# Second layer of a two-layer metaformer: the softplus chain, the convolution taps and the B/C eviction move to other steps of ScalarE's turn, and the gate's matmul uses the convolution's bank

## The reference, cut to what matters

```
xz = einsum('bhwc,ec->bhwe', xp, in_proj_w)          # x_in and x_gate, 96 channels each
x_act = silu(conv3x3_depthwise(x_in))                # two-dimensional
# _mamba(x_act):
xm, z = split(x_act @ in_w)                          # 96 channels each
xm = silu(conv1d_depthwise(xm, 3 taps) + c1_b)
dt_r, Bm, Cm = split(xm @ xp_w)
dt = softplus(dt_r @ dt_w + dt_b);  A = -exp(A_log)
h[t] = exp(dt*A) * h[t-1] + (dt*xm) * Bm             # 16 states per channel
y = (sum over states of h*Cm + xm*D) * silu(z)
out = einsum((y @ out_w) * silu(x_gate), out_proj_w)
```

## Time and profile before

| | |
|---|---|
| median of 3 runs | 1864.99 us (1864.54 to 1865.83) |
| the profiled execution's own time | 1864.62 us |
| its span on the core | 1862.8 us |
| scans of the phase | first starts at 937.8 us, last at 1697.4 us |
| mean granted TensorE clock | 0.791 of full speed |

### The profile page before, as it was taken

How to read it: one execution, slowest core, us unless ns; L and a number is a source line. 1 busy time by engine, 2 the same in 40 slices (tenths; PEclk the granted TensorE clock), 3 DMA queues, 4 the chain that set the end, 5 groups by cost and what they waited for, 6 DMA issues and landing times. The chain is left out here.

```text
span 1862.8 us, 16204 instructions
## 1 busy us (share of the span) xinstructions
PE 1396.1 (75%) x4014; PEld 522.0 (28%) x4014; DVE 1346.9 (72%) x1217; ACT 1124.8 (60%) x1720; POOL 937.7 (50%) x430
## 2 busy tenths in 40 slices
PE   4499937455474188884888988888888888765996
PEld 3233300101001067762222222222222222110785
DVE  1255529999999445552078999999999999995575
ACT  3333327647476055563677888888887887741464
POOL 4100015958859300000387888888888888861000
PEclk9799955555555599996778888888888888865898
DMA  5323340020110213221466777767666667641562
GB/s 135 105 78 94 94 123 21 2 90 0 47 45 0 96 39 85 70 66 48 110 157 165 166 167 167 166 157 164 163 161 163 158 159 164 144 110 43 135 166 72
DMA packets 136006, 199.98 MB, mean 107 GB/s; under 512 B 27244, under 2 KB 69486, under 8 KB 134771
## 3 DMA queue, kind: packets, MB, share of 16 engines
q1 hardware_dynamic: 134522, 196.61, 42.1%
q10 hardware_dynamic: 1416, 2.61, 0.5%
HBM read 145.55 MB, written 53.63 MB: 107 GB/s over the span
## 5 line engine op out<-in xcount | busy, mean ns | idle before, releaser
L1650 DVE TENSOR_TENSOR_SCAN m_h<-m_qa,m_state,m_ub 128x512 f32<-128x512 f32 x384 | 464.0, 1262 | 53.9 <-ACT m_qa L1613 53.9
L1261 POOL TENSOR_TENSOR m_ub<-m_dlb,m_bt 128x1536 f32<-128x1536 f32 x128 | 439.1, 3439 | 17.4 <-DVE m_h L1650 14.4
L1613 ACT ACTIVATE m_qa<-m_dlb,k_a 128x512 f32<-128x512 f32 x384 | 250.3, 678 | 110.3 <-DVE m_h L1650 110.0
L1022 POOL TENSOR_TENSOR b_u<-b_dl,b_z 128x1024 f32<-128x1024 f32 x48 | 125.7, 2618 | 272.1 <-DVE b_dl L952 272.1
L1470 PE MATMUL m_qc<-m_bcr,k_selc 32*128 32x512 f32 x256 | 172.7, 759 | 83.4 <-DVE m_g L1661 83.3
L1661 DVE TENSOR_TENSOR m_g<-m_h,m_qc 128x1536 f32<-128x1536 f32 x128 | 222.4, 1737 | 15.2 <-DVE m_h L1650 8.8
L1486 PE MATMUL m_qy<-m_g,k_seld 128*32 128x512 f32 x768 | 170.3, 747 | 0.0
L887 PE MATMUL b_qc<-b_bc,k_pack_sel 96*128 96x512 bf16 x96 | 69.9, 824 | 127.3 <-DVE b_g L982 108.4
L1240 POOL MEMSET m_cva<- 128x640 f32 x2 | 1.3, 631 | 232.7 <-POOLq L1866 232.7
L968 DVE TENSOR_TENSOR_SCAN b_h<-b_da,b_h,b_u 128x1024 f32<-128x1024 f32 x36 | 118.0, 3278 | 0.0
L1405 PE MATMUL m_qf<-m_cva,k_conv 113*96 113x504 f32 (+1 forms) x192 | 94.9, 633 | 18.7 <-DMA m_cvb<-scratch_xpad 18.7
(11 more groups left out here) (179 smaller groups left out, 2804.2 us busy)
## 6 DMA issues: line engine op xcount, KB each, us to landing
m_dlb<-scratch_dldu SPq DMA_DIRECT2D x128, 384.0 KB, 10.2
m_bt<-scratch_brow SPq DMA_DIRECT2D x128, 256.0 KB, 6.0
scratch_dldu<-m_dldu SPq DMA_DIRECT2D x32, 384.0 KB, 3.1
scratch_z<-a_z SPq DMA_DIRECT2D x24, 256.0 KB, 4.5
b_z<-scratch_z SPq DMA_DIRECT2D x3, 2048.0 KB, 7.7
scratch_y<-b_yrow SPq DMA_DIRECT2D x3, 2048.0 KB, 6.3
c_y<-scratch_y SPq DMA_DIRECT2D x16, 384.0 KB, 3.3
scratch_gate<-m_gt SPq DMA_DIRECT2D x32, 192.0 KB, 5.0
```

Of the source, the lines that this page charges most:

```text
L1022: nc.gpsimd.tensor_tensor(by_column(u[s][:], col), by_column(dl[s][:], col), seen(z[:], col, piece), ALU.mult).then_inc(u_ready, 1)
L1261: nc.gpsimd.tensor_tensor(ub[k % 3][:], dlb[u % 2][:, J:2 * J, :], bcast(bt[u % 2][:, n, :], J), ALU.mult).then_inc(ub_ready, 1)
L1613: nc.scalar.activation(q_a[:, j, :], dlb[u % 2][:, j, :], ACT.Exp, scale=G["a1"][:, j, n:n + 1]).then_inc(da, 1)
L1650: nc.vector.tensor_tensor_scan(h[k % 3][:, j, :], q_a[:, j, :], ub[k % 3][:, j, :], state[:, k % NS, j:j + 1], ALU.mult, ALU.add).then_inc ...
```

## The change

The steps of the turn are dealt out anew. On ACT `log(t+3)` moves from s = 2 to s = 3, and `taps` and `rows_out` move from s = 3 of one turn to s = 0 of the next (so they are written with `t+3` and `t+2`), `rows_out` now ahead of `taps`. The SiLU of the gate moves behind the other three. The gate's matmul writes to `q_f`, the bank of the two-dimensional convolution, after its SiLU has read it (`xa_ready`), in place of `q_g`, the bank of `dt_of`. DVE's `softplus` moves from s = 0 to s = 1, ahead of `outputs`. POOL and SP follow with their parts.

```diff
 # POOL
             def step(t, s, k):
+                if s == 1:
+                    conv_sum(t + 3)
                 drive(k + 2)
-                if s == 3:
-                    rounding(t + 3)
                 if s == 0:
-                    conv_sum(t + 3)
-                if s == 1:
+                    rounding(t + 2)
+                if s == 2:
                     du_of(t + 2)
 # SP
             def step(t, s, k):
+                if s == 0:
+                    store_rows(t + 2)
                 if s == 1:
-                    store_drive(t + 2)
                     store_y(t - 1)
                     load_cv(t + 6)
                 if s == 2:
                     store_gate(t + 4)
+                    store_drive(t + 2)
                 if s == 3:
                     load_rows(t + 2)
                     load_drive(t + 2)
-                    store_rows(t + 3)
 # PE, conv_pairs, gate_of, dt_of
                 if v >= 1:
-                    pe.wait_ge(xa_ready, v)
+                    pe.wait_ge(gt_ready, v)
...
-                if v >= 1:
-                    pe.wait_ge(gt_ready, v)
-                if v >= 2:
-                    pe.wait_ge(delta, v - 1)
-                nc.tensor.matmul(q_g[:], G["l1_gate"][:], cva[v % 2][0:C, W:W + CH], start=True, stop=True).then_inc(gate_mm, 1)
+                pe.wait_ge(xa_ready, v + 1)
+                nc.tensor.matmul(q_f[:], G["l1_gate"][:], cva[v % 2][0:C, W:W + CH], start=True, stop=True).then_inc(gate_mm, 1)
...
-                pe.wait_ge(gt_ready, min(v + 2, UNITS))
+                if v >= 1:
+                    pe.wait_ge(delta, v)
                 nc.tensor.matmul(q_g[:], G["wdt"][:], xm[v % 4][:], start=True, stop=True).then_inc(dt_mm, 1)
 # ACT, window: the gate's SiLU behind sz and xm, from q_f
-                    act.wait_ge(gate_mm, a + 1)
-
-                    if a >= 2:
-                        act.wait_ge(gt_stored[a % 2], 16 * (a // 2))
-                    nc.scalar.activation(gt[a % 2][:], q_g[:], ACT.Silu).then_inc(gt_ready, 1)
...
+                if exists(a):
+                    act.wait_ge(gate_mm, a + 1)
+
+                    if a >= 2:
+                        act.wait_ge(gt_stored[a % 2], 16 * (a // 2))
+                    nc.scalar.activation(gt[a % 2][:], q_f[:], ACT.Silu).then_inc(gt_ready, 1)
 # ACT
                 if s == 2:
                     u_of(t + 4)
+                if s == 3:
                     log(t + 3)
-                if s == 3:
-                    taps(t + 4)
-                    rows_out(t + 3)
+                if s == 0:
+                    rows_out(t + 2)
+                    taps(t + 3)
 # DVE
             def step(t, s, k):
                 scans(k)
-                if s == 0:
+                if s == 1:
                     softplus(t + 2)
-                if s == 1:
                     outputs(t - 1)
                 times_c(k - 1)
```

## The result

| | before | after |
|---|---|---|
| median | 1864.76 us (1862.95 to 1865.83, 4 runs) | 1877.28 us (1875.42 to 1881.51, 4 runs) |
| profiled execution, its span | 1864.62, 1862.8 us | 1876.55, 1874.8 us |
| mean granted clock of the span | 0.791 | 0.781 |

The changed kernel takes 1.0071 times as long, 95% interval 1.0052 to 1.0090. It is slower, by 12.5 us where I had forecast 43.

The account below looks back on a forecast made before the run. DVE, nearest to full, was taken to be held by ACT's late decay. Removing that but delaying `z_of`, 22.04 + 1.30 + 2.0 for PE's clock gave 25.3 us a turn, 1.4 slower over 29 turns: 1908 us, range 1870 to 1945.

Parts of the forecast that it names:

- DVE's own turn of 22.04 us: On DVE, a turn's own work without waits was put at 22.04 us, against a measured turn of 23.88.
- The wait for the decay goes: Ahead of DVE's scans of s = 0, the wait of 1.00 to 1.68 us for ACT's decay was to disappear.
- At full clock the outputs wait 1.30 us for what hangs on `z_of`, turn 23.34: Later `rows_out` delays `z_of` and PE's queue through `add_up`, so DVE's outputs wait 1.30 us; turn 23.34 at 2.4 GHz.
- The rest costs nothing as long as its cover holds: The moved gate, POOL work and DMAs were to cost nothing; `gate_of` waits for `xa` a microsecond at most.
- PE's longest gap, 2.8 us, lies ahead of `z_of`, and the low stretch on the 4.98 us behind it: PE idles 2.8 us before `z_of`; 1.2 GHz then covers work through `add_up`, losing 2.0 us, turn 25.3.
- my own sign of being wrong: On PE, matmuls of `conv_low`, `c_of(0)` and `add_up` running at 2.4 GHz in most turns would refute the forecast.
- Rival 2: PE's clock stays up behind `z_of`, or falls ahead of `c_of(2)` over work with slack: turn 23.34, 1849 us, chance 0.12.
- Today this costs DVE little: In the kernel before, PE's 6.2 us a turn at 1.2 GHz lies over s = 2 work for which nobody waits.
- ACT's lateness: ACT starts the decay only behind `log`; 1.84 us of a turn are DVE's waits, mostly ahead of s = 0 scans.
- The rule on gaps: By the skill's page PE's clock would stay up, since harmful gaps are longer; the sum would then be turn 23.34.
- a gap of 2.11 us is enough: On PE, the trace before was read as showing that idling 2.11 us for `m_g` lowers the clock.
- Rival 5: `m_dlb` comes late, so POOL and ACT wait for a DMA, 2 us a turn: about 1925 us, chance 0.05.

## Why the prediction came out as it did

The sign was right, the size not: 1877 us lies in the range, but the loss is 12.5 us and not 43. The sign is in part luck, for the wait that makes the loss is not the one that I forecast.

- *DVE's own turn of 22.04 us*: right. Turns of 21.97 us occur as soon as nothing holds DVE.
- *The wait for the decay goes*: right. It is in no list of the changed kernel.
- *At full clock the outputs wait 1.30 us for what hangs on `z_of`, turn 23.34*: right as a statement on the order, shown by the turn of 23.17 us with 1.13 in the run with spare work (PE idles 2.5 us ahead of `z_of` in it). In the changed kernel itself the wait is 0.34 us, since DVE has by then been held 1.26 us for `c_of(2)` and 0.31 for the next one.
- *The rest costs nothing as long as its cover holds*: this is the step that failed. I wrote of `gate_of` that it "waits a microsecond at most" and checked the slack of `c_of(1)` alone. It waits 1.96 us, the clock falls behind it, and the queue reaches `c_of(2)`, which I had starting at X + 0.23, as if nothing stood ahead of it. With X = 1227.73, the start of the scans of s = 3, it starts at 1231.40, X + 3.67, and DVE waits 1.47 us a turn for it. I followed the wait to the first instruction that somebody wants and stopped one short.
- *PE's longest gap, 2.8 us, lies ahead of `z_of`, and the low stretch on the 4.98 us behind it*: wrong, as a consequence. PE comes late from that queue and idles 0.27 us there, and `c_of(0)` and `add_up` take 1.12 and 1.06 us, at 2.4 GHz: my own sign of being wrong. The low stretch lies behind `gate_of`, up to `u_of` or `dt_of`. I took 2.0 us for it and a turn of 25.3; the loop gives 24.24.
- *Why the loss is smaller than forecast*: from `gate_of` to `c_of(2)` the queue has some slack at full clock (7.1 us in the run with `z_of` behind; with 13.9 that is a loop of 21.0, one under DVE's 22.04), while the stretch that I feared has none. So a low stretch of 6.8 us lifts the turn only from 23.17 to 24.16 us, as two turns of the run with spare work show, and with the rarer turns of 25.8 the mean is 24.40 against 23.88 before. Rival 2 had the low stretch elsewhere as well, but over work with slack enough to hide it. Had the clock fallen behind `z_of`, more would have been lost: in the run with the gate in its own bank turns of 27.7 us occur, though the mean of its profiled execution is 24.8.
- *"Today this costs DVE little"*: wrong. The turns of the kernel before come in threes, two with 6.8 us low and one with about 3, and the one is 1.1 to 1.4 us shorter:

```profile
1285.01:1309.19 24.18, 21.44 (x55) 5.21 (x54) 22.15 (x20) 19.54 (x34) 19.86 (x10) 0.86 0.70 161
1309.19:1332.22 23.03, 20.30 (x55) 5.05 (x54) 22.03 (x19) 19.54 (x34) 19.86 (x10) 0.93 0.64 168
```

  They are the turns with the waits of 1.68 and 1.00 us for the decay in the earlier trace rows. So of the 1.84 us that I put down to ACT's lateness only 1.00 is there in every turn; the rest comes and goes with the length of the low stretch.
- *The rule on gaps*: the page TensorE: Matmul & The Clock Gate of the Trainium skill, "HAM oscillation", counts as harmful only gaps longer than any in the turns of these two kernels. By that rule the clock stays. The trace disagrees, as in the earlier trace rows: it falls behind a gap of 1.96 us in the changed kernel, and 0.89 was no protection in the run with `skip_of` ahead. But that "a gap of 2.11 us is enough", as I wrote, is not shown either, for the clock falls with no gap as well.
- *Rival 5*: its 1925 us does not follow from its terms. 2 us in place of the clock's loss is the turn of the forecast again, about 1907. No wait for a DMA appears, so nothing hangs on it.

What stays open is why the clock falls at a given place (in 12 us of unbroken work in one kernel, behind a gap of 0.89 us in another, and nowhere in a turn with 2.6 us of idle time in a third) and why it stays low as long as it does: stretches of about 3.4, 6.8, 10, 14, 17, 20 and 27 us occur. That PE's gap ahead of `gate_of` lowers it in the changed kernel is not shown: the fall comes within 1.6 us behind that gap in every turn, but in the run with spare work, where the gap is filled, the clock falls at the same place in about half of the turns. That it is the low clock and not the order of PE's queue that makes the turns long is shown by turns of one and the same kernel (23.17, 24.16 and 27.66 us with 0, 6.8 and 13.3 us low in one, 21.97 and 29.05 in another, 21.96 and 32.65 in a third), not by a run in which the clock alone was changed; such a run was not tried.

## What to carry to other kernels

Where one engine's queue is followed for a wait, follow it to the last instruction in it for which somebody else waits, at both levels of the clock, not to the first. Two late places in one loop can hide each other: an edit that relieves one shows almost nothing, so try them together (3 us, which is within the noise, 9 us, and 44 for both). Where a theory names a gap as the cause, fill the gap and look whether the effect goes; the total time alone does not tell. And before spending a bank change to save a wait, try it alone: here it cost 93 us by itself, and undoing it, with one reordering on PE, gave a kernel 1.6% faster than the one before.

## What the runs showed of the hardware

- The granted clock does not follow PE's busy time. It stayed at 1.2 GHz for 20 us in which PE was busy throughout, it fell from 2.4 to 1.2 GHz in the midst of 12 us without a pause, and it stayed at 2.4 GHz over a turn in which PE was idle for 23.17 - 20.57 = 2.6 us.
- The pattern of low stretches repeats over several turns. In the changed kernel every seventh turn takes 25.8 us and the others 24.1 to 24.2; in the one before every third takes 23.0 and the others 24.2 to 24.5. Edits that move one matmul changed the time by up to 109 us (`skip_of`, on top of the fastest kernel) in the direction opposite to the one intended. With such a kernel a change of order on PE has to be measured; its sign can't be had from the sum of durations.
